# A two-layer decoder on one core: loads and weight splits of the first element reordered, the last batch's projection spread over its pairs, side work of the recurrence moved to other steps

## The chip, the cores and the metric

One core of a Trainium2 chip runs the whole program. TensorE multiplies into banks of PSUM (2 KB a partition), VectorE, ScalarE and GpSimd read and write SBUF, the first two PSUM as well; transfers are issued by the sync engine's queue (SP) and can be by ScalarE's. The metric is device microseconds from start to end of the program, median of the runs.

## The reference

Two decoder layers on x [8, 256, 128] with context [8, 512, 128]; after every sublayer the sum with x is normalised.

```python
x = ln(x + L0_attn(x))            # 16 heads of 8, causal, window 64, relative bias, softmax
x = ln(x + L0_xattn(x, ctx))      # 16 heads of 64, rotary keys, scores clipped at 11, softmax
x = ln(x + L0_ffn(x))             # weight rounded to -1, 0, 1; x scaled by its peak
x = ln(x + L1_attn(x))            # recurrence over 256 tokens
x = ln(x + L1_xattn(x, ctx, ctx, mask))   # linear attention
x = ln(x + L1_ffn(x))             # fp8-rounded x and weight

def step(state, inp):             # the recurrence of L1_attn
    u_t, sp_t = inp
    state = jnp.tanh(state @ A.T + u_t @ B.T) + sp_t
    return state, state @ C.T
```

## The kernel before

Each engine has one program, written out in order; semaphores tie them. The order is by hand: a step that waits holds all that stands behind it on its engine.

**First element** (start to line 2032 on TensorE). The loads (lines 501 to 540) are issued by SP one after the other. `rel`, the relative bias, is transposed, copied to `rel_row`, written to a DRAM scratch (line 513) and read back as `bias_mask`, four transfers (line 519). `x`, `w_qkv` and `w_proj` (`w_nat`) are transposed; `q0`, `k0`, eight masked copies `km` and `vm` follow. Scores of eight head pairs (`first_scores`, `first_score`, line 1251) go through two pairs of banks; ScalarE takes the exponentials (`exps_of`, line 867); probabilities are turned by TensorE in twelve jobs, even ones copied by ScalarE (`even_turn`), odd ones by VectorE (`odd_turn`, line 1321), and weighed into `o0`, which VectorE divides (`S_DIVIDE`, line 1271). `S_PROJ` makes y, `S_X1` x1, `S_LATN` the latents `lat`, `S_LAT` their split. Beside it the context is turned (`ctx_t`), normalised (`cn`), turned and split; its key/value products (`products_of_ctx`) are measured (`measure_kv`) and scaled (`keep_kv`). cos and sin are spread and turned (`prepare_trig`, `keep_cos`, `sin_t`).

fp32 products of the cross-attention are made from a high and a low part of each operand. The weights are split once: ScalarE copies the high part (`split_high`, lines 925 to 933), GpSimd subtracts it (`split_low`, line 697), four weights of 1024 columns. TensorE waits for all of them before the first keys.

**Batches.** Eight batches of eight head pairs. In a pair: scores in two units (line 2133), exp, clamp on VectorE (line 1471), `values_of` (line 2057), sums of the four exp tiles on GpSimd (lines 731 to 735), `sum_of` (line 2065), reciprocal and product on VectorE (`attended`, lines 1373 and 1374), and GpSimd's `rotate` of the keys (line 641). Keys, queries and values of later pairs are made by jobs whose PSUM bank `number_jobs` gives: "p" and a second bank by `SECOND_BANK`, in turns; pair 3 has none, so all its jobs go through "p". In batches 0 to 6 the self-attention of the next batch runs in slots between. In the last batch `beside_last_batch` prepares the tail's matrices and each batch's f (`normalize_f`, `turn_f`, `keep_f`); the output projection of the last batch stands behind it (lines 2189 to 2205).

**Tail and recurrence.** f is quantised, multiplied, x3 normalised in four parts (`add_product`, `normalize_x3`). Two are turned and give the first 64 steps of z (`begin_z`); the others are made beside the recurrence (`late_work`), as is the rest of z in thirds from step `LATE_Z` on. A step is 2 x 2 matmuls of 8 columns and a tanh. Windows of 16 steps carry the following sublayers (`window`; on VectorE `rectify_queries`, line 1584). Steps that have nothing else get a `keep_clock` matmul of 192 or 96 columns.

## Time and profile before

| | us |
|---|---|
| runs: lowest, median, highest of 3 | 1046.6, 1050.55, 1050.72 |
| profiled execution | 1047.62 |
| its span, first to last instruction | 1045.9 |
| first element | 0 to 57.9 |
| eight batches | 57.9 to 812.1 |
| tail before the recurrence | 812.1 to 839.7 |
| recurrence, 255 steps | 839.7 to 988 |
| rest | 988 to 1045.9 |

TensorE is busy 88% of the span, VectorE 65%, ScalarE and GpSimd 49% each. The mean granted TensorE clock is 0.944; a clock of 0.5 in a stretch is 1.2 GHz, one of 1.00 is 2.4 GHz. The shares are averages over stages with different limits; a saving is read from the waits inside a stage.

### The profile page before, as it was taken

The page shows a single profiled execution, that of the slowest core. Times are in us where ns is not written, and L with a number is a line of the kernel's source. Part 1 is how long each engine was busy: PE and PEld are TensorE (multiplying, and loading weights), DVE is VectorE, ACT ScalarE, POOL GpSimd, SP SyncE. Part 2 cuts the span into 40 slices and gives each one's busy share as a digit, 9 for nine tenths or more (in the row PEclk, how much of TensorE's full clock was granted, in tenths as well). Part 3 has the DMA queues.
Part 4 walks back from the last instruction along what each step waited for, and adds up shares of the span by engine and source line. Part 5 has one row for each costly group of instructions (what it writes and reads, how often), then busy time and mean ns, then how long its engine had stood idle before and what let it go on. Part 6 is the DMA issues. An engine that isn't in the chain of part 4 may idle for free.

```text
span 1045.9 us, 22097 instructions
## 1 busy us (share of the span) xinstructions
PE 919.8 (88%) x8504; PEld 652.6 (62%) x8504; DVE 681.3 (65%) x1906; ACT 509.6 (49%) x1441; POOL 510.7 (49%) x642
## 2 busy tenths in 40 slices
PE   6689989998999999899989999998988499999922
PEld 4456656666665756566666666666656379888721
DVE  6446577568757766776687577667689543444477
ACT  6655645653663556456636645564233023333324
POOL 2643475356546534654565466446657112333363
PEclk9989999999999989999999999999999589999955
DMA  7000000000000000000000000000000001222211
...
DMA packets 60470, 15.09 MB, mean 14 GB/s; under 512 B 41278, under 2 KB 59726, under 8 KB 60238
## 3 DMA queue, kind: packets, MB, share of 16 engines
...
q14 instruction: 36, 0.29, 0.1%
...
## 4 chain that ended last, share of the span: by engine, by line
PE 64%; DVE 19%; ACT 7%; POOL 5%; issue 3%; DMA 1%; SPq 0%; POOLq 0%; DVEq 0%; ACTq 0%
PE score_banks L2133 10%; PE out_bank L2057 8%; PE score_banks L1758 5%; DVE o_rec L1373 5%; PE bank_a L1753 5%; PE score_banks L2071 4%; DVE prob L1471 3%; PE score_banks L1789 3%; PE score_banks L1760 3%; PE score_banks L1759 3%; PE score_banks L2261 3%; PE bank_d L1774 3%; PE out_bank L2040 2%; PE out_bank L2065 2%; PE bank_d L2274 2%
## 5 line engine op out<-in xcount | busy, mean ns | idle before, releaser
L1007 ACT ACTIVATE prob<-score_banks 128x1024 f32<-128x1024 f32 x128 | 131.0, 1024 | 165.8 <-PE score_banks L2133 165.5
L733 POOL TENSOR_TENSOR psum<-psum,prob 128x512 f32<-128x512 f32 x64 | 81.6, 1275 | 153.9 <-DVE prob L1471 153.9
L2133 PE MATMUL score_banks<-qh,kr 64*128 64x256 f32 x1024 | 150.9, 415 | 2.1 <-ACT qh L916 1.3
L731 POOL TENSOR_TENSOR psum<-prob 128x512 f32<-128x512 f32 x64 | 82.6, 1290 | 98.4 <-DVE prob L1471 98.3
L1373 DVE RECIPROCAL o_rec<-out_bank 128x256 f32<-128x256 f32 x64 | 111.9, 1748 | 26.1 <-PE out_bank L2065 26.0
L2057 PE MATMUL out_bank<-prob,v 128*64 128x256 f32 x1024 | 124.7, 386 | 1.4 <-DVE on L1374 1.4
L2133 PEld LDWEIGHTS score_banks<-qh,kr 64*128 64x128 f32 x1024 | 91.9, 193 | 40.7 <-issue 30.5
L867 ACT ACTIVATE prob<-prob,neg_max 128x128 f32<-128x128 f32 (+1 forms) x256 | 107.1, 426 | 13.5 <-DVE neg_max L1258 13.5
L1471 DVE TENSOR_SCALAR prob<-prob 128x1024 f32<-128x1024 f32 x128 | 101.4, 792 | 12.9 <-ACT prob L1007 12.9
L2057 PEld LDWEIGHTS out_bank<-prob,v 128*64 128x64 f32 x1024 | 67.9, 136 | 46.6 <-issue 17.2
L1056 ACT ACTIVATE prob<-score_banks 128x8 f32<-128x8 f32 x255 | 45.1, 177 | 96.1 <-PE score_banks L2261 96.1
L1315 DVE TENSOR_TENSOR k_cos<-score_banks,cos_t 128x512 f32<-128x512 f32 x56 | 38.2, 682 | 72.4 <-PE score_banks L1760 46.2
L641 POOL TENSOR_TENSOR kr<-k_cos,k_sin 128x512 f32<-128x512 f32 x64 | 82.8, 1294 | 4.4 <-DVE k_sin L1317 3.6
L735 POOL TENSOR_TENSOR psum<-psum,prob 128x512 f32<-128x512 f32 x64 | 81.6, 1275 | 3.9
L2261 PE MATMUL score_banks<-prob,pt 128*64 128x8 f32 x1020 | 74.3, 210 | 0.6 <-ACT prob L1053 0.3
L835 ACT ACTIVATE pt<-bank_a 128x512 f32<-128x512 f32 x84 | 50.2, 598 | 35.5 <-PE bank_a L1753 34.6
L1774 PE MATMUL bank_d<-km,q 64*128 64x128 f32 x480 | 50.6, 330 | 17.9 <-DVE row_max L1253 16.6
L2261 PEld LDWEIGHTS score_banks<-prob,pt 128*64 128x64 f32 x1020 | 53.4, 137 | 20.8 <-ACT prob L1056 14.5
L2071 PE MATMUL score_banks<-w_qkv_t,ident 128*64 128x96 f32 (+1 forms) x336 | 64.8, 277 | 0.0
L1753 PE MATMUL bank_a<-ident,prob 128*128 128x128 f32 x360 | 57.0, 281 | 4.0 <-ACT pt L835 2.3
L1789 PE MATMUL score_banks<-pt,vm 128*32 128x128 f32 x768 | 54.0, 281 | 4.5 <-ACT pt L938 3.8
L760 POOL TENSOR_TENSOR var_eps<-mv,epsilons 128x1 f32<-128x1 f32 x49 | 9.5, 194 | 96.1 <-DVE mv L1575 96.1
...
## 6 DMA issues: line engine op xcount, KB each, us to landing
...
```

Of the source, the lines that this page charges most:

```text
L641: g.tensor_tensor(kr[:, key % 2, :], k_cos[:, :], k_sin[:, :], ALU.add).then_inc(kr_ready, 1)
L731: link(g.tensor_tensor(psum[:, p % 2, :], pp[:, 0, :], pp[:, 1, :], ALU.add))
L867: last = s.activation(pr, pr, ACT.Exp, bias=neg_max[:, qt, j, g:g + 1], accum_out=row_sum[:, qt, j, g:g + 1])
L1007: s.activation(prob[:, p % 2, 2 * u:2 * u + 2, :].rearrange("p k (h q) -> p h k q", h=2), sc[:, 0:2, :].rearrange("p h (k q) -> p h k q", ...
L1373: link(w.reciprocal(o_rec[:, :], bank[:, T:2 * T]))
L1471: w.tensor_scalar(pr, pr, float(np.exp(-CLIP)), float(np.exp(CLIP)), ALU.max, ALU.min).then_inc(clamped, 1)
L1753: return nc.tensor.transpose(out_ap, in_ap, ident[0:in_ap.shape[0], 0:in_ap.shape[0]])
L1789: last = mm(o0_bank[32 * g:32 * g + 32, qt * P:(qt + 1) * P], vm[:, kt, j, 32 * g:32 * g + 32], pt[:, t % 2, i * P:(i + 1) * P], start=(j ...
L2057: mm(o[DH * h:DH * (h + 1), 0:T], v[:, (q // 2) % 2, kb, lo:lo + DH], prob[:, q % 2, kb, T * h:T * (h + 1)], start=(kb == 0), stop=(kb == ...
L2071: mm(bank[0:HALF_ROWS, 0:columns], ident[:, 0:HALF_ROWS], w_qkv_t[:, 0:columns], start=True, stop=True, skip_group_check=True)
L2133: last = mm(sc[:, h, k * T:(k + 1) * T], kr[rows_of, p % 2, kb * P:(kb + 1) * P], qh[rows_of, p % 2, :], start=True, stop=True, skip_group ...
L2261: last = mm(cf[lo:lo + HALF_ROWS, t * B:(t + 1) * B], a_t[:, lo:lo + HALF_ROWS], hid[:, (t - 1) * B:t * B], start=False, stop=True, skip_g ...
```

## The change

In the first element: the identity is made first and TensorE waits for it alone; w_qkv and w_proj are issued by ScalarE; the scratch write and its read-back come before most loads, cos and sin behind the large weights; the high parts of all weights and the low parts of `wq` and `wv` are made by VectorE, the keys' low parts by GpSimd; TensorE waits for the keys' parts before keys and for the others before values; first jobs use five banks; scores run ahead of the context's work, and the key/value sum ahead of the second values. `prob1`'s zeros are written by GpSimd, `ctx_t` by VectorE. In the last batch all second banks are "o0"; the output of pair p - 2 is added up in pair p; the last two adds of the last pair's sum are VectorE's. Ahead of the recurrence the second part of x3 is turned into its own bank before z begins. In the recurrence the late products start at step 9 and 18 instead of 3 and 10, the late turns at 26 and 42 instead of 17 and 25, and z's thirds go to the steps of `Z_STEPS`; VectorE's late parts move accordingly, and keep_clock follows whether a step carries work.

```diff
+FIRST_BANKS = ("p", "d2", "s0", "s1", "o", "p", "s0")
 SECOND_BANK = ("o0", "o0", "o0", None, "d2", "d2", "o0", "o0")
...
+bank = fixed or (second if second and bank == "p" else "p")
...
-        add((b, p, kind), kind, target, SECOND_BANK[p])
+        add((b, p, kind), kind, target, SECOND_BANK[p] if b < B - 1 else "o0")
...
+LAST_D2_JOB = [j.done for j in JOB.values() if j.bank == "d2"][-1]
+FIRST_LATE = 9
+Z_EARLY = (13, 14, 15, 22, 30, 38, 46, 54, 58, 60, 61, 62)
+Z_STEPS = [*Z_EARLY, *(t for t in range(64, T) if t % WINDOW_STEPS in (10, 12, 13, 14))][:3 * Z_PARTS]
-    load(w_nat[:, 0:3, :], a["L0_attn_w_qkv"].rearrange("(k p) c -> p k c", p=P), signal=qkv_in)
-    load(w_nat[:, 3, :], a["L0_attn_w_proj"], signal=qkv_in)
...
+    sp.wait_ge(d_free, 1)
+    sp.dma_start(scratch, rel_row).then_inc(scratch_out, 16)
+    row("L0_attn_b_proj", b_proj, signal=proj_in)
...
     col("L0_xattn_ln_ctx_b", CTX_B, signal=ctx_cols_in)
...
     sp.wait_ge(scratch_out, 16)
+    load(keep[:, :, :], a["mask_BxS2_ff1"].rearrange("b (k p) -> p b k", p=P), slow=True, signal=keep_in)
     load(wkv_nat, a["L0_xattn_Wkv"], signal=split_in)
     load(wq_nat, a["L0_xattn_Wq"], signal=split_in)
+    load(trig_nat[:, 0], a["L0_xattn_cos"].rearrange("(k p) d -> p k d", p=P), signal=trig_in)
+    load(trig_nat[:, 1], a["L0_xattn_sin"].rearrange("(k p) d -> p k d", p=P), signal=trig_in)
+    link(g.memset(ident[:, :], 0.0))
+    g.affine_select(out=ident[:, :], in_=ident[:, :], compare_op=ALU.not_equal, fill=1.0, base=0,
+                    pattern=[[-1, P]], channel_multiplier=1).then_inc(ident_ready, 1)
...
+    g.memset(prob1[:, :, 0:WINDOW], 0.0).then_inc(zeros_ready, 1)
+        last = split_low(1, low, wkv_nat[:, 0:INNER].rearrange(swapped, t=2, d=HALF)[:, 1 - t], high)
+    last.then_inc(keys_split, 1)
-    split_low(2, wq_s[:, 1, :], wq_nat, wq_s[:, 0, :])
-    split_low(3, wv_s[:, 1, :], wkv_nat[:, INNER:2 * INNER], wv_s[:, 0, :]).then_inc(weights_split, 1)
...
+            if pair == B * PAIRS - 1:
+                first.then_inc(last_sum_begun, 1)
+                break
...
+        if k == 1:
+            rstd_of(NORMS, 3, 4, EPS_LN, half=1)
+    act.dma_start(w_nat[:, 0:3, :], a["L0_attn_w_qkv"].rearrange("(k p) c -> p k c", p=P)).then_inc(qkv_in, 16)
+    act.dma_start(w_nat[:, 3, :], a["L0_attn_w_proj"]).then_inc(qkv_in, 16)
...
-    act.wait_ge(ctx_full, 1)
-    s.activation(ctx_t[:, :], bank_p[:, :], ACT.Identity).then_inc(ctx_kept, 1)
-    act.wait_ge(trig_full, 2)
-    s.activation(sin_t[:, :], sc[:, 1, :], ACT.Identity, scale=sign[:, 0:1]).then_inc(sin_kept, 1)
     apply_norm(0).then_inc(cn_ready, 1)
+    exps_of(0, 0, 0, 1)
+    exps_of(0, 1, 0, 2)
+    even_turn(0)
     act.wait_ge(ctx_cols_in, 16 * 2)
     act.wait_ge(cn_full, 1)
...
-    exps_of(0, 0, 0, 1)
-    keep_kv(0, 0)
-    exps_of(0, 1, 0, 2)
-    even_turn(0)
+    s.activation(cn_raw_first[:, :], bank_p[:, :], ACT.Identity, **by_feature)
+    s.activation(cn_s[:, 0, 0, :], bank_p[:, :], ACT.Identity, **by_feature).then_inc(cn_kept, 1)
     exps_of(0, 1, 1, 2)
     even_turn(2)
-    split_high(0)
     exps_of(0, 2, 0, 2)
     even_turn(4)
     exps_of(0, 2, 1, 2)
-    split_high(1)
+    keep_kv(0, 0)
     exps_of(0, 3, 0, 2)
     even_turn(6)
     exps_of(0, 3, 1, 2)
+    act.wait_ge(trig_full, 2)
+    s.activation(sin_t[:, :], bank_d2[:, :], ACT.Identity, scale=sign[:, 0:1]).then_inc(sin_kept, 1)
+    even_turn(8)
     keep_kv(0, 1)
-    even_turn(8)
-    split_high(2)
     even_turn(10)
-    split_high(3)
...
-                    bank_a[:, :].rearrange("p (b t) -> p b t", b=4))
+                    (bank_a, ob)[k][:, :].rearrange("p (b t) -> p b t", b=4))
+        dve.wait_ge(split_in, 16 * 2)
+        if part == 0:
+            last = w.tensor_copy(wk_s[:, 0, :], wkv_nat[:, 0:INNER])
+        if part == 1:
...
+    def split_low(part):
+        dve.wait_ge(weights_high, part + 1)
+        full, t = ((wq_nat, wq_s), (wkv_nat[:, INNER:2 * INNER], wv_s))[part - 2]
+        w.tensor_tensor(t[:, 1, :], full, t[:, 0, :].bitcast(F32), ALU.subtract).then_inc(weights_split, 1)
...
-    prepare_trig()
-    centre_weights()
-    keep_cos()
-    dve.wait_ge(scratch_out, 16)
-    w.memset(prob1[:, :, 0:WINDOW], 0.0)
-    measure_kv(0, 0)
+    dve.wait_ge(ctx_full, 1)
+    w.tensor_copy(ctx_t[:, :], bank_p[:, :]).then_inc(ctx_kept, 1)
     for at in range(6):
         first_score(at)
     odd_turn(1)
     first_score(6)
     first_score(7)
+    centre_weights()
     odd_turn(3)
+    measure_kv(0, 0)
+    split_high(0)
+    split_high(1)
+    odd_turn(5)
+    prepare_trig()
+    self_attention(0, S_CN, 0)
+    split_high(2)
+    odd_turn(7)
+    keep_cos()
     measure_kv(0, 1)
-    odd_turn(5)
-    self_attention(0, S_CN, 0)
-    odd_turn(7)
+    split_high(3)
+    split_low(2)
     odd_turn(9)
     invert_sums(0)
     odd_turn(11)
     self_attention(0, S_DIVIDE, 0)
+    split_low(3)
     self_attention(0, S_PROJ, 0)
     first_keys("a", 0)
+    self_attention(0, S_RELU, 0)
     self_attention(0, S_X1, 0)
     first_keys("b", 0)
     self_attention(0, S_LATN, 0)
     first_keys("a", 1)
     self_attention(0, S_LAT, 0)
-    self_attention(0, S_RELU, 0)
     first_keys("b", 1)
     self_attention(0, S_KV_SUM, 0)
...
+            def add_last_sums():
+                dve.wait_ge(last_sum_begun, 1)
+                dve.wait_ge(clamped, 2 * pair + 2)
+                link(w.tensor_tensor(psum[:, p % 2, :], psum[:, p % 2, :], prob[:, p % 2, 2, :], ALU.add))
+                w.tensor_tensor(psum[:, p % 2, :], psum[:, p % 2, :], prob[:, p % 2, 3, :],
+                                ALU.add).then_inc(last_sum_ready, 1)
...
-    add_product(0)
-    add_product(1)
+    measure_x3(0, *add_product(0))
+    measure_x3(1, *add_product(1))
     normalize_x3(0)
     normalize_x3(1)
     quantize_f(2)
     quantize_f(3)
-    add_product(2)
-    normalize_x3(2)
-    add_product(3)
+    measure_x3(2, *add_product(2))
...
         if k == 1:
+            normalize_x3(2)
+            product_3 = add_product(3)
+        if k == 2:
             normalize_x3(3)
-            keep_late(0)
...
         normalize_window(W_Q, q1, bank_d[:, 0:D]).then_inc(q_ready, 1)
+        if k == 2:
+            keep_late(1)
         if k == 1:
-            keep_late(1)
+            measure_x3(3, *product_3)
+            keep_late(0)
-    first_scores(0)
-    pe.wait_ge(kv_centred, 1)
+    for at in range(3):
+        first_scores(at)
     pe.wait_ge(ctx_kept, 1)
-    products_of_ctx(0, bank_p)
-    first_scores(1)
     pe.wait_ge(cn_ready, 1)
     for k in range(KB):
-        last = turn(ob[:, k * P:(k + 1) * P], cn[:, k, :])
+        last = turn(bank_p[:, k * P:(k + 1) * P], cn[:, k, :])
     last.then_inc(cn_full, 1)
-    for at in range(2, 6):
+    for at in range(3, 6):
         first_scores(at)
+    pe.wait_ge(zeros_ready, 1)
...
+    first_turn(3)
+    first_weigh(2)
+    pe.wait_ge(kv_centred, 1)
+    pe.wait_ge(cn_kept, 1)
+    products_of_ctx(0, bank_p)
+    for at in range(4, 7):
+        first_turn(at)
+        first_weigh(at - 1)
+    pe.wait_ge(trig_ready, 1)
+    pe.wait_ge(d_free, SETUP_D + D_SCORE + 7)
+    for t, bank in enumerate((bank_d, bank_d2)):
+        for k in range(KB):
+            last = turn(bank[:, k * P:(k + 1) * P], trig_rep[:, t, k].rearrange("p r d -> p (r d)"))
+        last.then_inc(trig_full, 1)
+    first_turn(7)
+    first_weigh(6)
     pe.wait_ge(kv_free, 1)
     products_of_ctx(1, bank_p)
-    for at in range(3, TURNS):
+    for at in range(8, TURNS):
         first_turn(at)
         first_weigh(at - 1)
...
-    pe.wait_ge(weights_split, 1)
+    pe.wait_ge(keys_split, 1)
     pe.wait_ge(cn_split, 1)
     pe.wait_ge(kv_free, 2)
     prep_keys(JOB["keys a", 0], 0, "a")
+    pe.wait_ge(cos_kept, 1)
     self_attention(0, S_PROJ)
+    pe.wait_ge(sin_kept, 1)
     prep_keys(JOB["keys b", 0], 0, "b")
-    for half in range(2):
-        prep_values(JOB[f"values {half}", 0], 0, half)
-    prep_keys(JOB["keys a", 1], 0, "a")
-    prep_keys(JOB["keys b", 1], 0, "b")
+    pe.wait_ge(weights_split, 2)
+    pe.wait_ge(d_free, SETUP_D + D_SCORE + 8)
+    prep_values(JOB["values 0", 0], 0, 0)
+    self_attention(0, S_KV_SUM)
+    prep_values(JOB["values 1", 0], 0, 1)
     pe.wait_ge(weights_in, 16 * SETUP_LOADS)
     pe.wait_ge(lat_ready, 1)
     for qt in range(QT):
         last = turn(bank_a[:, qt * P:(qt + 1) * P], lat[:, qt, :])
     last.then_inc(a_full, 1)
+    pe.wait_ge(odd_free, TURNS // 2)
+    prep_keys(JOB["keys a", 1], 0, "a")
+    prep_keys(JOB["keys b", 1], 0, "b")
     pe.wait_ge(lat_split, 1)
     prep_queries(JOB["queries", 0], 0)
-    self_attention(0, S_KV_SUM)
...
     def beside_last_batch(p):
+        if p == 2:
+            engine, count = LAST_D2_JOB
+            pe.wait_ge(p_free[engine], count)
+        if p >= 2:
+            output_of_last(p - 2)
...
     values_of(B * PAIRS - 1)
+    sum_of(B * PAIRS - 1)
+    output_of_last(PAIRS - 2)
+    turn_f(B - 2)
+    output_of_last(PAIRS - 1).then_inc(y_full, 1)
...
-            last = turn(bank_a[:, i * P:(i + 1) * P], x3_tok[k][:, i, :])
+            last = turn((bank_a, ob)[k][:, i * P:(i + 1) * P], x3_tok[k][:, i, :])
+    turn_x3(0)
+    turn_x3(1)
     begin_z(0)
     begin_z(1).then_inc(c_ready, 1)
-        for k, first in ((2, 3), (3, 10)):
+        worked = False
+        for k, first in ((2, FIRST_LATE), (3, FIRST_LATE + 9)):
...
-        for k, first in ((2, 17), (3, 25)):
+        for k, first in ((2, 26), (3, 42)):
...
-        if LATE_Z <= t < LATE_Z + 3 * Z_PARTS:
-            part, third = divmod(t - LATE_Z, 3)
+        if t in Z_STEPS:
...
         if not worked:
-            keep_clock(KEEP_Z if busy else KEEP, spare)
-        elif not busy and i not in (0, 6):
+            keep_clock(KEEP_Z if worked_late or t < FIRST_LATE else KEEP, spare)
+        elif i not in (0, 6) and t > WINDOW_STEPS:
             keep_clock(KEEP_Z, spare)
```

## Rows read from the trace of the kernel before

**Rows 1.** Stages: length, busy us and instructions by engine, then PEclk, DMA, GB/s.
```profile
0.00:57.90 57.90, 37.91 (x291) 26.59 (x291) 32.10 (x144) 35.11 (x109) 24.84 (x51) 0.97 0.38 97
...
812.10:839.70 27.60, 14.73 (x45) 10.21 (x45) 14.05 (x54) 2.79 (x4) 4.22 (x8) 0.51 0.00 0
839.70:846.30 6.60, 6.41 (x64) 5.85 (x64) 1.21 (x4) 1.51 (x9) 0.00 (x0) 0.50 0.01 2
```

**Rows 2.** Timeline, bias: start, us, engine, line, operation; landing of `bias_mask`.
```profile
5.87 0.43 SPq L513 DMA_DIRECT2D bias_scratch<-prob  x1
...
8.95 1.87 SPq L519 DMA_DIRECT2D bias_mask<-bias_scratch  x1
...
DMA to landing us min/median/max: 4.7/5.4/6.1
...
16.18 0.26 DVE L1251 CUSTOM_DVE_ANT_0 prob<-bank_d,bias_mask 128x128 f32<-128x128 f32 x1
```

**Rows 3.** Chain of waits, end of the weight splits: start us, us, engine, line.
```profile
39.05 0.95 ACT wq_s L931
...
42.40 2.35 POOL wv_s L697
```

**Rows 4.** Timeline, from `o0` to the first unit; in brackets idle time before.
```profile
42.80 0.42 DVE L1271 TENSOR_TENSOR o<-score_banks,rec_t 128x256 f32<-128x256 f32 x1 [0.81 <-PE score_banks L1789]
46.25 0.42 DVE L1276 TENSOR_TENSOR y<-bank_d,xbp 128x256 f32<-128x256 f32 x1 [3.03 <-PE bank_d L1880]
...
51.08 0.60 DVE L1190 TENSOR_SCALAR lat<-x,mv,rstd 128x128 f32<-128x128 f32 x2 [0.51 <-POOL rstd L626]
...
54.17 0.60 PE L1753 MATMUL bank_a<-ident,lat 128*128 128x128 f32 x2
...
56.86 1.10 PE L1888 MATMUL bank_d<-v,k 128*128 128x130 f32 x8
```

**Rows 5.** Two lines, last batch: ns min/median/max, starts; then the cn split.
```profile
L1190 DVE TENSOR_SCALAR lat<-x,mv,rstd x8: 342/1161/1423, 752.0 to 804.5; 128x128 f32<-128x128 f32 x8
...
L1471 DVE TENSOR_SCALAR prob<-prob x15: 674/682/684, 739.6 to 803.6; 128x1024 f32<-128x1024 f32 x15
...
31.46 0.68 DVE L1305 TENSOR_TENSOR cn_s<-k_sin,cn_s 128x512 fp32r<-128x512 f32 x1
```

**Rows 6.** Timeline, TensorE in pairs 1 and 3 of the last batch.
```profile
752.17 0.38 PE L1758 MATMUL score_banks<-wv_s,cn_s 128*128 128x256 f32 x1 [0.88 <-DVE k_sin L1317]
...
769.39 0.38 PE L1758 MATMUL score_banks<-wv_s,cn_s 128*128 128x256 f32 x1 [1.16 <-DVE k_sin L1317]
...
772.77 2.08 PE L2133 MATMUL score_banks<-qh,kr 64*128 64x256 f32 x8
```

**Rows 7.** Timeline, end of the last batch, TensorE and VectorE.
```profile
805.64 3.39 PE L2196 MATMUL bank_d<-wo,on 128*128 128x128 f32 x28
...
809.88 1.76 DVE L1373 RECIPROCAL o_rec<-out_bank 128x256 f32<-128x256 f32 x1 [0.53 <-PE out_bank L2065]
```

**Rows 8.** Timeline, x3 to z, TensorE.
```profile
831.17 1.12 PE L1753 MATMUL bank_a<-ident,cb 128*128 128x128 f32 x4 [3.42 <-DVE cb L1190]
...
837.56 1.22 PE L2238 MATMUL score_banks<-prob,pt 128*128 128x256 f32 x2 [1.17 <-ACT prob L990]
```

**Rows 9.** Timeline, tanh steps on ScalarE: steps 4, 26 and 32 of the recurrence.
```profile
842.62 0.18 ACT L1056 ACTIVATE prob<-score_banks 128x8 f32<-128x8 f32 x1 [0.78 <-PE score_banks L2261]
...
857.00 0.18 ACT L1056 ACTIVATE prob<-score_banks 128x8 f32<-128x8 f32 x1 [1.02 <-PE score_banks L2261]
...
861.16 0.18 ACT L1056 ACTIVATE prob<-score_banks 128x8 f32<-128x8 f32 x1 [0.59 <-PE score_banks L2261]
```

**Rows 10.** Timeline, first window of the recurrence: VectorE, then the first attend on TensorE.
```profile
857.57 0.41 DVE L1578 TENSOR_SCALAR psum<-bank_d,mv,rstd 128x128 f32<-128x128 f32 x1 [0.94 <-POOL rstd L762]
...
860.09 0.41 DVE L1584 TENSOR_SCALAR psum<-bank_a,cols 128x128 f32<-128x128 f32 x1 [0.56 <-PE bank_a L2269]
...
861.52 0.39 PE L2297 MATMUL out_bank<-psum,km 128*64 128x16 f32 x8
```

136 lines of the change are left out of this document (63 added, 73 removed).

## The prediction

> **What bounds the kernel now.** I read the busy shares first, then the stages, then the chain of waits inside each stage that the change touches, then the single instructions on it. No engine is the bound over the whole span; the stretches have different limits, and the change edits four of them.
>
> The first element runs from 0 to 57.9 us, with TensorE busy only 37.9 us of it [rows 1]. Its chain starts with the bias table: the scratch row is written at 5.87, read back as `bias_mask` from 8.95, landed 4.7 to 6.1 us after each issue, and the first score is read at 16.18 [rows 2]. It goes on with the splitting of weights: ScalarE's copy for `wq_s` (0.95 us), then GpSimd's 2.35 us for `wv_s`, before which TensorE starts no keys [rows 3]. `o0` is divided at 42.80, y waits 3.03 us for its product, `lat` is ready at 51.7, and its transpose starts at 54.17, queued behind values and keys; 1.10 us of key/value sum stand directly ahead of the first unit at 57.9 [rows 4].
>
> The seven batches from there to 742 are hardly touched. In the last batch pair 3 has all its projections in bank "p" in a row: TensorE stands still 1.16 us for `k_sin` and falls to the low clock, so that the next unit takes 2.08 us for its 8 matmuls [rows 6]. From 812.1 to 839.7 TensorE is at 0.51 of its clock and waits for the other engines [rows 1]. The recurrence is ScalarE and TensorE in turns: 255 steps in the 148.3 us from 839.7 to 988. A plain step is 0.565 us, its 0.18 on ScalarE and 0.39 of waiting; 255 of them would be 144.1, so 4.2 us are lost in a few steps (three of them in [rows 9]).
>
> **The change part by part.** The sum is made against the profiled execution: 1047.62 us, of which the span is 1045.9. The median of the three runs is 1050.55, 2.9 us higher; the saving is taken to be the same for both.
>
> *First element, head.* `ident` comes first on GpSimd, w_qkv and w_proj are issued from ScalarE's queue (two issues, 0.43 us each by the SP rows), and the scratch write moves ahead of eight issues, so it goes out at about 3.6 instead of 5.87 [rows 2]. The read-back follows 3.1 us later as before, at 6.7, and lands at 11.4 to 12.8. VectorE's work ahead of the scores, now with the `ctx_t` copy but without trig, weight centring, memset and first key/value statistics, ends near 11. The first score is then read at 12.0, 4.2 us earlier, and all exponentials move up by as much.
>
> *First element, splits.* ScalarE loses four copies of 1024 columns, VectorE gets them. SBUF to SBUF with one source it takes 0.68 us for 1024; with two sources 0.68 for 512 [rows 5]. I take 0.68 each (one source, both sides in SBUF) and keep 1.36 as the upper bound; the two low parts taken from GpSimd have two sources, 1.2 to 1.4 us each. From its first key/value statistics (ending at 26.6 by this schedule) to the division VectorE now has four turn evacuations (2.4), trig (0.7), the cn split (0.6), four high parts (2.7), one low part (1.2), cos (0.6), statistics (1.3) and the inversion (1.8): 11.3 us, and some 2.2 us in which it waits for TensorE's order: 40.1. VectorE, not the splits on GpSimd, is the new bound here.
>
> What adds to that is the neighbour. The 128-column normalisations of `lat` take 342 ns alone and up to 1423 ns while GpSimd adds [rows 5]: such a pass waits for a GpSimd instruction to end. GpSimd's low parts of the keys (two of 2.35 us [rows 3]) now run beside prepare_trig and the high parts. Between nothing and 3.2 us are lost, so the division lies between 40.1 and 43.3; I take 42.2, two thirds of the way, since only the seven one-source passes can be held and three or four of them meet a long GpSimd instruction. The Trainium skill (SBUF — State Buffer, "SBUF: two separate sides") says that VectorE's two-port passes, and also its passes with two sources in SBUF against a GpSimd instruction that reads SBUF, shut each other out for a whole instruction. The first half agrees with the 342 and 1423 ns. By the second half the moved low parts would be held too, the division would come at 43.3 and the total be 1.1 us higher.
>
> From the division to the first unit the kernel takes 57.9 - 42.8 = 15.1 us. The wait of y (3.03) is replaced by the last low part (1.2), since the product now finds its weights: -1.8. The 2.5 us in which `lat` waits behind values and keys go, and the sum of 1.10 us moves ahead of it; but `kr` for pair 0 and the next k_cos now stand before the split of `lat` on VectorE: +0.7. That leaves 10.4 [rows 4]. Saving of the stage: 4.7, and 0.6 from the earlier division: **5.3 us**; bounds 3.0 (all passes held, and once more behind the division) and 7.4.
>
> *Last batch.* With two banks in pair 3 the first values need not wait for `k_sin`, only the second, as in pair 1, where the wait is 0.88 us [rows 6]. The second values then end 2.3 us earlier. The output matmuls, 28 in 3.39 us [rows 7], cost 0.46 us a pair: on the path in pair 3, which leaves 1.9, and in pair 5 (0.46 more), hidden in the even ones, where GpSimd's adds and rotate end later than TensorE. Without the low clock the unit takes 1.13 rather than 2.08, which wins up to 0.95; I take it whole. The 3.39 us that leave the end save nothing by themselves: the last reciprocal waited only 0.53 us for TensorE [rows 7], so VectorE was free at 809.35. It now does the last two adds (1.36 us) and wins 0.93 where GpSimd no longer holds its normalisation: free at 809.8, no gain. Stage: 1.9 + 0.95 - 0.46 - 0.2 = **2.2 us**, the 0.2 being what is hidden less than fully; bounds 1.0 and 3.2.
>
> *Between batch and recurrence.* The first x3 transpose starts at 831.17 and the second half of z only at 837.56, since transpose and copy of the second half stand between; the first tanh comes at 839.7 [rows 8]. With a bank of its own the second transpose runs beside the first copy and ends at 833.8, then both halves of z follow at 2.07 us each: 838.0. **1.6 us**, bounds 1.2 and 1.8.
>
> *Recurrence.* Four steps with side work at the low clock last 0.96 us, the others there 0.67. Moving it to step 9 saves 4 x 0.29 = 1.2 us, less if the clock rises later than 6.4 us after the first step. The step with 1.02 us of idle (waiting for x3) becomes a plain one: 0.64. Three window starts that carry z as well lose 0.22 each (0.59 idle for 0.39), five smaller ones 0.2 together [rows 9]. Against it: behind the first q (normalised at 857.98) VectorE has statistics of x3 (1.25), keep_late (1.0) and the w8 copy (0.15) ahead of rectify_queries (1.06): 861.45. The first attend started at 861.52, 0.35 us behind its input; with 0.64 and 0.22 less before it, it would start at 860.66 and so stalls 0.8 [rows 10]. 1.2 + 0.64 + 0.65 + 0.2 - 0.8 = **1.9 us**; bounds 0.8 and 2.9.
>
> The sum: 5.3 + 2.2 + 1.6 + 1.9 = **11.0 us**. That is 1036.6 for the profiled execution and 1039.5 from the median; I predict 1038.
>
> **The rivals.** *VectorE is held throughout.* Every one-source pass beside GpSimd's splits waits, the first element saves 1 to 3 us: total 6 to 8, about 1042. For it the 1423 ns; against it that such passes are seven in a stretch of 15 us. By the skill's page above this is the rule rather than the exception.
>
> *Nothing is held.* GpSimd's splits fall between VectorE's passes: division at 40.1, and the clock rises early in the recurrence: 14 to 15 us, 1034.
>
> *Slower: the recurrence stays at the low clock.* Steps 1 to 8 now hold one 96-column keep_clock beside the 8-column matmuls and no side work; in the kernel before the clock rose right after the four steps that had it [rows 1, 9]. At the low clock a plain step costs 0.10 us more, one with side work 0.40. Of the first 64 steps 29 carry side work: 3.5 + 11.6 = 15.1 us, 2.0 of them paid today. The forecast holds 0.8 of it (eight steps). The gain of 11 is used up if the clock stays low to about step 50 (0.236 a step); if it stays so to step 100, with four side steps in sixteen, 36 x 0.175 = 6.3 come on top: 21.4, and 1038 + 20.6 = 1059. Against it: in the steps before the side work TensorE had no idle rows either.
>
> *The banks or the lifted order don't do what they say*: VectorE or GpSimd holds pair 3 anyway and the first unit waits for `rotate`; last batch and first element give under 2 us together: 1046, no change.
>
> **How the numbers follow.** Forecast (total 8.5 to 13): 0.50. VectorE held: 0.20. Nothing held: 0.13. Banks and order without effect: 0.12. Clock low past step 50: 0.05. Range 1030 to 1046: it takes in the first three cases, with the 2.9 us between profile and median on either side, and leaves out most of the last two. 0.5%, about what a measurement of this kernel can tell from no change, is 5.3 us: faster than 1045.3 holds 0.50 + 0.19 + 0.13 = 0.82; the same 0.13; slower 0.05.
>
> **What would show it.** First score near 12 us, division at 40 to 43, first unit at 51 to 54; a high part near 0.7 us alone and over 1.5 us beside GpSimd. In pair 3 no idle of over 1 us but one, and the next unit at 1.1 us; the last reciprocal released by VectorE itself. Both x3 transposes before the first z. From first unit to first tanh 778.0 us where it was 839.7 - 57.9 = 781.8. Steps 3 to 6 at 0.67 us, one longer step at 34. I am wrong if the first unit starts after 55.5, or if steps after the twelfth last 0.67 us or more.

## The result and the profile after

The changed kernel takes 1038.67 us, the median of five runs (1037.42 to 1040.2); the kernel before, run beside it, 1048.51 (1046.6 to 1050.72, five runs). The ratio is 0.9905, with a 95% interval of 0.9884 to 0.9926. The profiled execution took 1038.29 us, 9.3 less than that of before.

I cut both profiled executions at the same instructions, among them the reciprocals of the attention sums (one for each pair of each batch), and set the difference beside the forecast:

| stretch (us) | before | after | difference | forecast |
|---|---|---|---|---|
| start to reciprocal of pair 0, first batch | 76.40 | 71.72 | -4.68 | -5.3 |
| to reciprocal of pair 0, last batch | 672.31 | 672.88 | +0.57 | 0 |
| to reciprocal of pair 7, last batch | 61.17 | 58.87 | -2.30 | -2.2 |
| to the first tanh | 29.78 | 27.37 | -2.41 | -1.6 |
| first to last tanh | 148.34 | 147.78 | -0.56 | -1.9 |
| to the end | 57.90 | 57.88 | -0.02 | 0 |
| sum | 1045.90 | 1036.50 | -9.40 | -11.0 |

So the time is close to the 1038 forecast. The table alone doesn't say that the reasons hold; for the first row, they turned out not to. That row also reaches further than its forecast, which was made for the first unit of the cross-attention's scores: there the difference is 3.10 us (57.90 to 54.80). The other 1.58 arise in the next four microseconds, as these rows show, two from the kernel before and one from the changed one:

```profile
57.90 1.98 PE L2133 MATMUL score_banks<-qh,kr 64*128 64x256 f32 x8
60.40 0.63 PE L1759 MATMUL score_banks<-cn_s,wk_s 128*128 128x512 f32 x1
...
56.20 0.39 PE L1801 MATMUL score_banks<-cn_s,wk_s 128*128 128x512 f32 x1
```

The kernel before runs this stretch at half clock (58.0 to 61.4 us), the changed one doesn't; its first unit, shown below, takes 1.13 us.

The stages of the changed kernel (length, busy us and instructions of each engine, PEclk, DMA share, GB/s), to be read beside [rows 1]: before the recurrence TensorE is still at half its clock, and in its first ten microseconds it is again for most of the time.

```profile
0.00:54.80 54.80, 38.70 (x291) 28.16 (x291) 39.88 (x154) 30.31 (x102) 23.78 (x50) 0.97 0.41 102
54.80:738.00 683.20, 639.03 (x4844) 433.15 (x4845) 466.50 (x1208) 377.54 (x955) 364.60 (x373) 0.98 0.02 5
...
805.30:830.84 25.54, 14.29 (x45) 10.35 (x45) 14.42 (x54) 2.79 (x4) 4.21 (x8) 0.51 0.00 0
830.84:840.70 9.86, 9.29 (x100) 7.86 (x101) 0.93 (x2) 2.48 (x14) 0.00 (x0) 0.65 0.01 2
```

The timeline of the first element in the changed kernel, the rows that answer [rows 2, 4, 5]: first score, the split of cn and the cast of `wq_s`, GpSimd's subtractions beside them, division, y, first unit.

```profile
12.68 0.29 DVE L1249 CUSTOM_DVE_ANT_0 prob<-bank_d,bias_mask 128x128 f32<-128x128 f32 x1 [1.14 <-PE bank_d L1816]
...
29.70 2.84 DVE L1303 TENSOR_TENSOR cn_s<-k_sin,cn_s 128x512 fp32r<-128x512 f32 x1
32.46 1.75 DVE L1341 CAST wq_s<-prob 128x1024 fp32r<-128x1024 f32 x1
...
29.45 2.54 POOL L707 TENSOR_TENSOR wk_s<-prob,wk_s 128x1024 fp32r<-128x1024 f32 x1
31.95 3.40 POOL L707 TENSOR_TENSOR wkx_s<-prob,wkx_s 128x512 fp32r<-128x512 f32 x2
...
43.33 0.42 DVE L1269 TENSOR_TENSOR o<-score_banks,rec_t 128x256 f32<-128x256 f32 x1 [2.17 <-PE score_banks L1831]
...
45.66 0.42 DVE L1274 TENSOR_TENSOR y<-bank_d,xbp 128x256 f32<-128x256 f32 x1 [0.77 <-PE bank_d L1922]
...
54.80 1.13 PE L2201 MATMUL score_banks<-qh,kr 64*128 64x256 f32 x8 [0.56 <-ACT qh L936]
```

The first score moves up by 3.5 us, but the division comes 0.53 later than before: all that was won ahead of it is lost again in between (0.54 of it to half clock from 42.0 to 45.4 us, as the late bias below shows). The split of cn takes 2.84 us where it took 0.68.

From the last batch and the way to z, the rows that answer [rows 6, 8] (the last reciprocal, [rows 7], starts at 803.47 with no idle time in front):

```profile
765.29 0.38 PE L1800 MATMUL score_banks<-wv_s,cn_s 128*128 128x256 f32 x1 [0.72 <-DVE k_sin L1315]
...
824.92 1.12 PE L1795 MATMUL bank_a<-ident,cb 128*128 128x128 f32 x4 [3.42 <-DVE cb L1188]
826.44 1.12 PE L1795 MATMUL out_bank<-ident,k 128*128 128x128 f32 x4 [0.41 <-DVE k L1188]
827.35 1.12 PE L2297 MATMUL score_banks<-prob,pt 128*128 128x256 f32 x2
```

And from the recurrence, ScalarE's tanh instructions that answer [rows 9]: tanh 6, behind a plain step at half clock; tanh 10, behind one with side work; tanh 35, behind step 34, which waits for the first attend.

```profile
834.33 0.18 ACT L1053 ACTIVATE prob<-score_banks 128x8 f32<-128x8 f32 x1 [0.49 <-PE score_banks L2322]
...
837.29 0.18 ACT L1053 ACTIVATE prob<-score_banks 128x8 f32<-128x8 f32 x1 [0.78 <-PE score_banks L2322]
...
853.46 0.18 ACT L1053 ACTIVATE prob<-score_banks 128x8 f32<-128x8 f32 x1 [0.98 <-PE score_banks L2322]
```

### The profile page after: what moved, and what is told of

The parts are those of the page before. It is cut to its first block, busy times and chain, and to the rows that moved or that the text cites. A ratio compares the mean times of both kernels' runs of the same rounds, so it can differ in the third digit from the quotient of the medians.

```text
span 1036.5 us, 22193 instructions
## 1 busy us (share of the span) xinstructions
PE 916.3 (88%) x8550; PEld 657.1 (63%) x8550; DVE 689.3 (66%) x1915; ACT 505.2 (49%) x1434; POOL 507.1 (49%) x639
## 4 chain that ended last, share of the span: by engine, by line
PE 62%; DVE 21%; ACT 7%; POOL 5%; issue 4%; DMA 1%; POOLq 0%; SPq 0%; DVEq 0%; ACTq 0%
PE score_banks L2201 9%; PE out_bank L2110 8%; DVE o_rec L1400 5%; PE score_banks L1800 5%; PE bank_a L1795 4%; DVE prob L1498 4%; PE score_banks L2127 3%; PE score_banks L2322 3%; PE score_banks L1831 3%; PE bank_d L1816 3%; PE score_banks L1801 3%; PE score_banks L1802 3%; PE out_bank L2093 2%; PE bank_d L2335 2%; PE out_bank L2121 2%
## 5 line engine op out<-in xcount | busy, mean ns | idle before, releaser
L1004 ACT ACTIVATE prob<-score_banks 128x1024 f32<-128x1024 f32 x128 | 131.1, 1024 | 164.7 <-PE score_banks L2201 164.4
L750 POOL TENSOR_TENSOR psum<-psum,prob 128x512 f32<-128x512 f32 x63 | 80.2, 1273 | 152.9 <-DVE prob L1498 152.9
L752 POOL TENSOR_TENSOR psum<-psum,prob 128x512 f32<-128x512 f32 x63 | 80.3, 1275 | 3.8
L2127 PE MATMUL score_banks<-w_qkv_t,ident 128*64 128x96 f32 (+1 forms) x336 | 60.7, 264 | 0.0
L930 ACT ACTIVATE v<-score_banks 128x512 f32<-128x512 f32 x57 | 34.0, 596 | 46.0 <-PE score_banks L1802 45.2
```

What stands on the lines that cost most here:

```text
L1004: s.activation(prob[:, p % 2, 2 * u:2 * u + 2, :].rearrange("p k (h q) -> p h k q", h=2), sc[:, 0:2, :].rearrange("p h (k q) -> p h k q", ...
L2127: mm(bank[0:HALF_ROWS, 0:columns], ident[:, 0:HALF_ROWS], w_qkv_t[:, 0:columns], start=True, stop=True, skip_group_check=True)
```

## The experiments

All are edits of the changed kernel. Since executions of one kernel differ by 2 to 8 us, more than most single parts are worth, I read their traces at the cuts of the table; the medians stand beside them, and no median by itself decides between two of these edits, but for the fillers. Each reading is of one profile. For the first element I count from the first score to the reciprocal of pair 0, because the first score itself moves between 12.0 and 12.7, most of it with TensorE's speed ahead of it. The same first scores, in the changed kernel and in the first run below:

```profile
11.09 1.44 PE L1816 MATMUL bank_d<-km,q 64*128 64x128 f32 x8 [0.62 <-DVE vm L1238]
...
11.04 0.82 PE L1822 MATMUL bank_d<-km,q 64*128 64x128 f32 x8 [0.83 <-DVE vm L1232]
```

1.44 us is what these eight products also take in a recorded stretch at half clock (267.33 us in the changed kernel). PEclk shows 1.00 here in both profiles, so the half clock at the start of the program has to be read from the length of the products. In seven of the changed orders' profiles the products take 0.82 us and the first score comes at 11.99 to 12.39; in six, the changed kernel's among them, they take 1.44 and it comes at 12.53 to 12.70.

**Low parts of the keys on VectorE.**

```diff
-            split_low(0, wk_s[:, 1, :], wkv_nat[:, 0:INNER], wk_s[:, 0, :])
...
-                last = split_low(1, low, wkv_nat[:, 0:INNER].rearrange(swapped, t=2, d=HALF)[:, 1 - t], high)
...
             split_high(3)
-            split_low(2)
+            split_low(0)
+            split_low(1)
...
+            split_low(2)
             split_low(3)
```

> The changed kernel with the low parts of the key weights (one of 1024 columns, two of 512 in swapped order) on VectorE too, so that GpSimd subtracts nothing in the first element; VectorE does them behind the high part of the values, and the low part of the queries moves behind the division. Changed kernel: cn split 2.84 us, cast of wq_s 1.75 us, division 43.33, first unit 54.80, reciprocal of pair 0 at 71.72. Theory (VectorE's passes are held by GpSimd's subtractions): cn split 0.7 and cast 0.7, which gives back 3.2 us; 2.6 us of new subtractions take part of it, 1.2 of which is paid back by the moved query part: division near 41.5, y about 44.3, pair 0 near 70.3, total 1.4 us lower. Rival (they are held by something else, such as the weights' DMA or ScalarE): both stay at 2.8 and 1.8, division near 44.7, total 1 to 2 us higher.

Measured: 1039.79 us (ratio to before 0.9932, 0.9902 to 0.9961). The passes on VectorE's timeline:

```profile
29.02 0.68 DVE L1297 TENSOR_TENSOR cn_s<-k_sin,cn_s 128x512 fp32r<-128x512 f32 x1
29.63 0.68 DVE L1335 CAST wq_s<-prob 128x1024 fp32r<-128x1024 f32 x1
...
41.35 0.42 DVE L1263 TENSOR_TENSOR o<-score_banks,rec_t 128x256 f32<-128x256 f32 x1 [0.73 <-PE score_banks L1837]
```

The holding is GpSimd's: 2.84 and 1.75 become 0.68 and 0.68. Division, y and pair 0 came at 41.35, 43.96 and 69.66, close to what was expected. But of the 2.06 us at pair 0, 0.67 is the earlier first score, and 1.24 a stretch at half clock (42 to 45.5 us) which this profile lacks and that of the changed kernel has. From the first score to pair 0 it is 57.65 us, against 57.80 in a profile of the changed kernel's order without such a stretch (the kernel of the late bias, below). The 3.23 us given back pay for the added subtractions and for waits on TensorE (0.53 and 1.46 us), and no more: 0.15 of the 1.4 expected.

**Memsets in place of GpSimd's subtractions.**

```diff
-                return g.tensor_tensor(low, full, high.bitcast(F32), ALU.subtract)
+                return g.memset(low.bitcast(F32), 0.0)
```

> The changed kernel in which GpSimd's three subtractions for the low parts of the keys are memsets of the same tiles: the low parts of the keys are left out of the computation, and GpSimd reads no SBUF there. Theory (a GpSimd instruction that reads SBUF holds VectorE's passes): cn split and wq_s cast about 0.7 us each, division about 40.5 to 41.5, since the last turns and the inversion follow VectorE. Rival (any GpSimd instruction holds them): a pass that meets a memset takes up to 1.6 us. Rival (not GpSimd): 2.84 and 1.75 stay. First unit by the theory 2 to 3 us earlier than 54.80, total 1035.5 to 1037 by the median.

Measured: 1038.29 us (0.9921, 0.9893 to 0.9949); division 41.13, first score to pair 0 56.73 us, without a stretch at half clock; that is 1.07 less than 57.80, the length with the subtractions and no such stretch. GpSimd's and VectorE's timeline:

```profile
28.83 0.95 POOL L707 MEMSET wk_s<- 128x1024 f32 x1
29.72 1.26 POOL L707 MEMSET wkx_s<- 128x512 f32 x2
...
28.42 2.10 DVE L1144 COPY v<-v 128x512 f32<-128x512 f32 x2
30.44 0.67 DVE L1303 TENSOR_TENSOR cn_s<-k_sin,cn_s 128x512 fp32r<-128x512 f32 x1
31.03 0.68 DVE L1341 CAST wq_s<-prob 128x1024 fp32r<-128x1024 f32 x1
```

The theory was half right. The split of cn, two sources in SBUF, runs in 0.67 us beside the second memset, though a subtraction held it for 2.2 us. The copy of one source ahead of it takes 2.10 us for its two instructions instead of 0.75: a memset holds that one. So what GpSimd does decides which passes it holds. The Trainium skill (SBUF — State Buffer, "SBUF: two separate sides") states just this pair of rules: one-source copies in the two-port mode exclude any GpSimd access, two-source passes only a GpSimd instruction that reads SBUF. Both halves agree with these rows.

**The bias later.** First behind five issues more on SP's queue, then behind nine.

```diff
-            sp.wait_ge(d_free, 1)
-            sp.dma_start(scratch, rel_row).then_inc(scratch_out, 16)
             row("L0_attn_b_proj", b_proj, signal=proj_in)
...
+            sp.wait_ge(d_free, 1)
+            sp.dma_start(scratch, rel_row).then_inc(scratch_out, 16)
             sp.wait_ge(scratch_out, 16)
```

> The changed kernel with the scratch write of the bias behind five more issues on SP's queue (b_proj, the two key/value weights, two columns), as it was in the kernel before: 2.3 us later. Theory (VectorE's queue of work carries a later first score to the division): first score near 15.0 instead of 12.68, division 45.3 to 45.7, pair 0's reciprocal 2 to 2.3 us later, total 2.2 us up. Rival (the division is set by the held passes and GpSimd's statistics, so that the early bias is worth nothing): division within 0.5 us of 43.33, total unchanged.

Measured: 1038.05 us (0.9905, 0.9878 to 0.9932). The write moved by 1.2 us only, since SP had waited for its row until 3.5 us anyway; first score 12.67, division 42.79, pair 0 70.47. This profile has no stretch at half clock in the first element, and so gives its undisturbed length: 57.80 us from first score to pair 0 (57.81 in the profile of the outputs at the end, which has none either). The second kernel:

> The changed kernel with the scratch write of the bias behind nine more issues on SP's queue, 3.6 us later than now, and its read-back as well. (One us later left the first score at 12.67: TensorE's product, not the bias, was last.) Now the bias lands near 15, as in the kernel before (16.1). Theory (VectorE's queue carries it on, less the 1.7 us in which it waits between 13 and 26): first score 15 to 16, division 44.0 to 44.8 where it is 42.8 without a stretch of low clock, pair 0's reciprocal 71.5 to 72.5 instead of 70.5. Rival (nothing of the early bias reaches the division): 42.8 and 70.5.

Measured: 1039.3 us (0.9902, 0.9875 to 0.9929); write at 6.62, read-back at 8.61, nearly as late as in the kernel before (8.95), and the first score:

```profile
12.39 0.29 DVE L1249 CUSTOM_DVE_ANT_0 prob<-bank_d,bias_mask 128x128 f32<-128x128 f32 x1 [0.53 <-PE bank_d L1816]
```

Still 12.39, and it waits for TensorE. First score to pair 0 is 58.93 us, with one stretch at half clock, where the changed kernel has 59.04, with one too. Both theories had the first score later and were wrong in that: with the read-back only 0.34 us ahead of its old place, the score still waits for TensorE, so loading the bias first brings nothing here. VectorE's timeline in the kernel before shows what held it there:

```profile
13.08 0.69 DVE L1165 COPY cos_t<-score_banks 128x512 f32<-128x512 f32 x1
13.93 0.91 DVE L1337 MEMSET prob<- 128x1024 f32 x1 [0.16 <-issue]
14.95 0.89 DVE L1176 BATCH_NORM_STATS2 stats<-score_banks 128x6 f32<-128x128 f32 x4
15.88 0.38 DVE L1179 BATCH_NORM_AGGREGATE mv<-stats 128x2 f32<-128x6 f32 x4
```

From 10.00 to the first score at 16.18 VectorE works with one pause of 0.16 us and waits for no load. The 3.5 us come from the other work that the change takes from in front of the scores: from 11.20 to 16.18 all is such work, and the copy of `ctx_t` that comes in its place takes 0.68.

**Low parts of queries and values back on GpSimd.**

```diff
             self_attention(0, S_KV_SCALE[1], 0)
+            split_low(2, wq_s[:, 1, :], wq_nat, wq_s[:, 0, :])
+            split_low(3, wv_s[:, 1, :], wkv_nat[:, INNER:2 * INNER], wv_s[:, 0, :]).then_inc(weights_split, 2)
...
-            split_low(2)
...
-            split_low(3)
```

> The changed kernel with the low parts of the query and value weights back on GpSimd, behind the second key/value scale, and the high parts still on VectorE. Theory (they are off the path either way, since TensorE starts the values only at 46.2): GpSimd ends them at 44.2, y is not behind a subtraction on VectorE any more, division 42.5 to 43 without a stretch at half clock (43.3 with one), pair 0's reciprocal within 0.7 us of 70.5 (71.7 with one). Rival (taking them from GpSimd was what made the first element faster): GpSimd's affine of the keys and the root for y come 4.7 us later, pair 0's reciprocal at 73 or later.

Measured: 1037.22 us (0.9891, 0.9861 to 0.9921); division 41.33, pair 0 at 69.71, 57.64 us behind the first score with one stretch at half clock: 1.4 us less than the changed kernel's 59.04. Better than the theory, and the opposite of the rival. Of the 1.4 us, 0.86 lie ahead of the division, which comes 29.26 us behind the first score here and 30.12 in the late bias, neither with a recorded stretch at half clock in between; the rest assumes that one stretch at half clock costs the same in both profiles. GpSimd does the two in time it has to spare, while VectorE's subtraction for the queries (1.22 us) stands on the path to the division. The one behind the division costs less: in the changed kernel VectorE still waits 0.77 us for TensorE after it.

```profile
37.96 2.35 POOL L707 TENSOR_TENSOR wq_s<-prob,wq_s 128x1024 fp32r<-128x1024 f32 x1
40.26 2.37 POOL L707 TENSOR_TENSOR wv_s<-prob,wv_s 128x1024 fp32r<-128x1024 f32 x1
```

**Pair 3 of the last batch with one bank.**

```diff
-                add((b, p, kind), kind, target, SECOND_BANK[p] if b < B - 1 else "o0")
+                add((b, p, kind), kind, target, SECOND_BANK[p] if b < B - 1 or p == 3 else "o0")
```

> The changed kernel with pair 3 of the last batch using bank p alone, as before. From reciprocal of pair 2 to that of pair 3: 12.18 us in the kernel before, 9.41 in the changed one. Theory (the second bank takes away the wait for k_sin): 9.41 + 1.9 = 11.3 us, 12.2 if TensorE also falls to half its clock there; total 1.9 to 2.8 up. Rival (the gain came from VectorE's last sums or from the output products' new places): it stays at 9.4.

Measured: 1040.45 us (0.9914, 0.9887 to 0.9941). From pair 2 to pair 3 11.13 us, against 9.41: the second bank is worth 1.72. The other 1.05 of the 2.77 is the half clock, which this profile doesn't have there, less what the output product in this pair costs. TensorE's waits in the pair:

```profile
764.06 0.50 PE L1800 MATMUL score_banks<-cn_s,wkx_s 128*128 128x512 f32 x1 [0.85 <-ACT qh L936]
...
765.81 0.39 PE L1800 MATMUL score_banks<-wv_s,cn_s 128*128 128x256 f32 x1 [0.78 <-DVE k_sin L1315]
...
767.47 0.39 PE L1800 MATMUL score_banks<-wv_s,cn_s 128*128 128x256 f32 x1 [0.69 <-ACT v L930]
```

**The output products at the end again.**

```diff
-                if p >= 2:
-                    output_of_last(p - 2)
...
-            sum_of(B * PAIRS - 1)
-            output_of_last(PAIRS - 2)
+            for p in range(PAIRS - 1):
+                output_of_last(p)
             turn_f(B - 2)
+            sum_of(B * PAIRS - 1)
```

> The changed kernel with the output products of the last batch at its end, ahead of the last sums, as before; the last two sums stay on VectorE. Theory (28 products cost 0.46 us in pairs 3 and 5, where TensorE is last; at the end they are hidden behind VectorE, which is busy until 803.5, nearly wholly): pair 3 8.95 us instead of 9.41, pair 5 8.07 instead of 8.53, last pair 8.3 to 8.9: total 0.9 lower to 0.3 lower. Rival (the 3.4 us in a row at the end delay the last sums): last pair 8.29 + 2 or more, total 1 to 2.5 us higher.

Measured: 1037.56 us (0.9892, 0.9855 to 0.9929). Pairs 3 to 7 take 9.24, 8.13, 8.08, 7.18 and 8.44 us, together 41.07; in the changed kernel 9.41, 8.23, 8.53, 7.18 and 8.29, together 41.64. Spreading the products costs 0.57 us: 0.45 in pair 5, 0.17 in pair 3, where half a microsecond was expected in each, and 0.10 in pair 4, with 0.15 won back in the last.

**x3 through one bank.**

```diff
-                    last = turn((bank_a, ob)[k][:, i * P:(i + 1) * P], x3_tok[k][:, i, :])
+                    last = turn(bank_a[:, i * P:(i + 1) * P], x3_tok[k][:, i, :])
...
             turn_x3(0)
+            begin_z(0)
             turn_x3(1)
-            begin_z(0)
             begin_z(1).then_inc(c_ready, 1)
```

> The changed kernel with both x3 transposes through bank_a, the second behind the first half of z, as before. From the last reciprocal to the first tanh: 29.78 us before, 27.37 in the changed kernel, where 1.6 of it was forecast for this edit. Theory (the edit is all of it, its size was underestimated because z's first half starts beside the second transpose): 29.5 to 29.9. Rival (0.8 of the 2.4 comes from elsewhere, such as the clock rising before the first step): 28.8 to 29.1.

Measured: 1041.59 us (0.9925, 0.9887 to 0.9963); last reciprocal to first tanh 29.95 us, 2.58 more than in the changed kernel. The edit accounts for the whole 2.41, and its size was underestimated.

**x3's statistics behind the queries.**

```diff
                 if k >= 2:
                     rectify_queries(k - 2)
+                if k == 2:
+                    measure_x3(3, *product_3)
+                    keep_late(0)
                 dve.wait_ge(pre_full, k)
```

> The changed kernel with the statistics of the last x3 part and the first keep_late behind rectify_queries of window 0 instead of ahead of it. Theory (these two, 2.3 us, make the first attend wait): the step at t = 34, now 1.15 us, becomes 0.57 to 0.70, and no other step grows: 0.5 us less from first to last tanh (147.78 now), total 0.5 lower, within the noise of the median. Rival (the wait goes elsewhere, to the window's x4 statistics, which now come behind them): step 34 is plain and a step between 35 and 42 grows by as much.

Measured: 1039.89 us (0.9922, 0.9891 to 0.9953). Step 34 is plain, 0.56 us; step 39 takes 1.38 instead of 0.56, since the transpose of x4 now waits for a normalisation that comes behind the 2.3 us:

```profile
857.27 0.44 PE L2331 MATMUL bank_a<-ident,v 128*64 128x128 f32 x4 [0.71 <-DVE v L1615]
...
857.99 0.18 ACT L1053 ACTIVATE prob<-score_banks 128x8 f32<-128x8 f32 x1 [1.21 <-PE score_banks L2323]
```

The rival was right: the wait only moves.

**192 columns in the first steps.**

```diff
-                    keep_clock(KEEP_Z if worked_late or t < FIRST_LATE else KEEP, spare)
+                    keep_clock(KEEP_Z if worked_late else KEEP, spare)
```

> The changed kernel with 192 instead of 96 columns in keep_clock in steps 1 to 8 of the recurrence. In the changed kernel the steps start at the full clock, it falls after step 5 (834 us), steps 6 to 9 last 0.67, the four with side work 0.96, and it rises behind these. Theory (the light steps let it fall): no fall, all of steps 1 to 16 at 0.56 to 0.58, first to last tanh 147.78 - 2.1 = 145.6 us. Rival (it falls on account of the idle time before the recurrence, whatever the steps hold): it falls at the same place, 147.8, and up to 0.1 more for each 192-column step at half clock.

Measured: 1036.76 us (0.9882, 0.9852 to 0.9913); first to last tanh 145.65 us. The first 16 steps all last 0.56 to 0.57, the four with side work too; the one that ends here lasted 0.96 in the changed kernel:

```profile
835.50 0.18 ACT L1053 ACTIVATE prob<-score_banks 128x8 f32<-128x8 f32 x1 [0.39 <-PE score_banks L2322]
```

The theory holds: the 96-column steps let the clock fall. The end took 1.0 us longer (58.87). The clock falls 4.1 us behind the last tanh here, 8.9 in the changed kernel, and by the statistics that follow the first products at half clock (5.70 us behind the last tanh, for 5.03) that accounts for 0.67 of it.

**TensorE's idle time in the batches filled.**

```diff
+FILL_SUM, FILL_SCORE = 6, 5
...
+                    if at == 1:
+                        a_job(A_CN + 1)
+                        for _ in range(FILL_SCORE):
+                            mm(bank_a[0:DH, 0:T], ident[:, 0:DH], w_qkv_t[:, 0:T], start=True, stop=True,
...
+                if q == PAIRS - 2:
+                    for _ in range(FILL_SUM):
+                        mm(ob[0:DH, T:2 * T], ident[:, 0:DH], w_qkv_t[:, 0:T], start=True, stop=True,
```

> The changed kernel with idle TensorE time in the batches filled: five 64x256 matmuls that nobody reads into bank_a ahead of the wait for the scores of slot 8 (2.07 us idle), six into the free half of the output bank ahead of the wait for the last partial sums in pair 6 (2.39 us idle). In the changed kernel's profile TensorE runs at half its clock six times between 60 and 740 us, for 3.4 or 6.8 us, each time behind one of these two waits; batches measured from pair 1 to pair 1 last 95.2 us without such a stretch and 96.5 to 98.3 with it. Theory (idle TensorE time causes the stretches, and they are also what makes executions differ by up to 4 us): no stretch is left, every batch takes 95.2, reciprocal of pair 1 to that of the last batch's pair 0 652 us instead of 660.6, total 1030, executions within 2 us of each other. Rival (they come from something else than these waits): stretches stay, 660, total 1038 or more where the fillers run at half clock.

Measured: 1028.32 us (0.9801, 0.9769 to 0.9833). First the changed kernel, six batches from pair 1 to pair 1, then the one wait and the filler that takes its place, then two of the six batches with fillers:

```profile
84.00:179.20 95.20, 89.31 (x692) 60.64 (x694) 66.35 (x174) 53.55 (x136) 51.66 (x53) 1.00 0.02 5
179.20:277.10 97.90, 92.15 (x692) 62.50 (x692) 66.36 (x173) 53.65 (x136) 51.66 (x53) 0.97 0.02 5
277.10:373.90 96.80, 90.92 (x692) 61.39 (x694) 66.64 (x174) 53.53 (x136) 51.83 (x53) 0.98 0.02 5
373.90:469.10 95.20, 89.31 (x692) 60.64 (x694) 66.33 (x174) 53.55 (x136) 51.66 (x53) 1.00 0.02 6
469.10:565.60 96.50, 90.74 (x692) 61.79 (x694) 66.41 (x174) 53.65 (x136) 51.67 (x53) 0.98 0.02 5
565.60:663.90 98.30, 92.41 (x692) 62.98 (x694) 66.55 (x174) 53.76 (x136) 51.70 (x53) 0.97 0.01 4
...
527.46 0.65 PE L2121 MATMUL out_bank<-psum,ones 128*64 128x256 f32 x4 [2.39 <-POOL psum L752]
```

```profile
519.91 2.75 PE L2124 MATMUL out_bank<-w_qkv_t,ident 128*64 128x256 f32 x12
522.47 0.65 PE L2131 MATMUL out_bank<-psum,ones 128*64 128x256 f32 x4
...
178.40:273.60 95.20, 93.89 (x714) 63.52 (x714) 66.39 (x173) 53.45 (x136) 51.72 (x53) 1.00 0.02 6
273.60:368.80 95.20, 93.90 (x714) 63.53 (x714) 66.40 (x173) 53.45 (x136) 51.73 (x53) 1.00 0.02 5
```

Without fillers four batches of six are 1.3 to 3.1 us longer than 95.2, at a mean clock of 0.97 or 0.98 and with the same work in every other engine. With them all six last 95.2 at 1.00. From pair 1 to the last batch's pair 0 that is 652.06 us instead of 660.63. The theory holds for the batches. It doesn't for the executions, which still ranged from 1026.2 to 1031.8. In the last batch the fillers only cost: it takes 61.03 us for 58.87. They remove idle time and add columns at once, and no run separates the two.

**Three edits together**: the low parts of all weights on VectorE, the fillers (not in the last batch), 192 columns.

> The changed kernel with three edits at once: all low parts on VectorE; the idle time of TensorE in the batches filled, but not in the last batch, where the six fillers cost 2.5 us in front of pair 6's sums and gave 0.3 back; 192 columns in the first steps of the recurrence. Theory (the three add up): pair 0's reciprocal 69.7 (70.5 to 71 if a stretch at half clock falls into the first element), batches 95.2 each, last batch as in the changed kernel, first to last tanh 145.6, total 1024 (1028.3 less 2.2 for the last batch, 2.1 for the recurrence, 0.8 for VectorE, plus 0.9 for the tail, which grew when the recurrence was faster). Rival (the half clock removed in one place comes back in another, since it follows something other than idle time): 1029 or more.

Measured: 1027.89 us (1025.34 to 1028.27, ratio 0.9798, 0.9767 to 0.9829). Batches 652.06, first to last tanh 145.66 and the last batch 58.86, all as expected. Two parts weren't: pair 0 at 71.47, with a stretch at half clock in the first element and the first score at 12.70, and 59.71 from last tanh to the end, 1.8 us more than in the changed kernel. The clock now falls 4.4 us behind the last tanh, but that is 0.4 of it: `att_scratch` is written 6.64 us behind the last tanh for 6.24. It is read back 3.01 us later, where the changed kernel needs 1.54, and this transfer is the rest. Stage and transfer:

```profile
966.60:1026.30 59.70, 18.07 (x189) 12.70 (x185) 40.41 (x140) 18.59 (x43) 26.81 (x54) 0.54 0.13 27
...
973.23 0.32 SPq L585 DMA_DIRECT2D att_scratch<-on  x1
976.24 0.37 SPq L588 DMA_DIRECT2D prob<-att_scratch  x1
```

So it gives 1028 and not 1024, by the medians the same as the fillers alone: what the profile shows lost is a stretch at half clock in the first element and a slow transfer, and only 0.4 us is half clock that comes back behind the recurrence, as the rival had it. Its median is the lowest of all, 0.4 us below the fillers alone and 2% below the kernel before. The subtractions of queries and values, better left on GpSimd, were not tried in it.

## Why the prediction was right

**First element: the number near in part by luck, the reasons mostly wrong.** *Size.* The 5.3 us were forecast for the first unit, which gains 3.10, at the forecast's lower bound of 3.0. The 4.68 of the table is near 5.3 only because the kernel before ran at half clock just behind that unit and the changed one did not: 1.58 us that no term of the sum held. Half clock ahead of the unit blurs the 3.10 too. The changed kernel has one stretch there, which costs 1.24 us (54.80 against 53.56 in the late bias); the kernel before has one as well, from 51.2 to 54.6, which can have cost up to half of its 3.4 us. As an estimate from these figures, the change itself is worth 2.6 to 4.3 us at the first unit. The medians, over five executions each, differ by 9.8 us, which is why the total stands all the same; its division into stretches hangs on the two profiles.

*Head.* Forecast 4.2 us for the first score, measured 3.5; the missing 0.6 is the half clock at the start, since with the products at 0.82 us the first score comes at the forecast 12.0. But the cause put first, the bias table, is not it. The prediction read "landed 4.7 to 6.1 us after each issue, and the first score is read at 16.18" as a chain, with no row that showed VectorE idle in front of that score. There was none: it had no idle time. The work taken from VectorE, which the prediction names beside it, was the cause.

*Splits.* The division was forecast at 42.2 and came at 43.33, or 42.79 without a stretch at half clock. GpSimd holds VectorE for 2.16 us in the split of cn and 1.07 in the cast, 3.23 together: the upper bound of 3.2, not the two thirds that I took. The prediction excluded the two-source pass from being held, and by the section of the Trainium skill that it cited it should not have. The rival "VectorE is held throughout" was right in this term, and with it the first element was to save 1 to 3 us: the 3.10 at the first unit doesn't tell it from the forecast, and without the 1.58 the profiles would differ by 7.8 us in all, within that rival's 6 to 8 and below the forecast's 8.5 to 13.

*Behind the division.* From there to the first unit 11.47 us, or 10.77 in the profile of the late bias, where 10.4 was forecast. Moving query and value parts to VectorE, which I counted as a gain ("the product now finds its weights"), costs up to 1.4 us.

**Last batch: right in mechanism and sum.** Pair 3 gave 2.77 us where 1.9 + 0.95 was forecast. Its parts are off and cancel: the bank gave 1.72 where 2.3 was said, and the output product costs 0.17 there and not 0.46. Pair 5 lost 0.45, as forecast, and the last reciprocal waits for VectorE's own queue. The prediction saw that spreading the output products wins nothing by itself; the experiment gives 0.57 us as their price.

**x3 to z: mechanism right, size off.** 2.41 for 1.6, above the bound of 1.8. The sum let both halves of z follow the second transpose, 2 x 2.07 us; in the trace the first half starts at 827.35, while the second transpose is ending, and four products take 3.5 us.

**Recurrence: a term failed.** The step was "moving it to step 9 saves 4 x 0.29 = 1.2 us". The four steps still last 0.96 us: the clock, high at the start, falls in step 5 (833.9 us) and rises only with the side work, so that the first 16 steps take 11.30 us instead of 11.06. The rival "the recurrence stays at the low clock" had the mechanism, that light steps don't hold the clock; it was wrong on how long, since the side work raises it. The Trainium skill (TensorE: Matmul & The Clock Gate, "What's actually happening") says that the throttled state is the default and that activity releases it; the run with 192 columns agrees, with 2.1 us saved. The other terms held: the step that waited for x3 (1.20 us) is gone, the starts of three windows lost 0.22 each, and the new stall at step 34 is 0.58 where 0.8 was forecast.

**What the sum left out.** In the batches between, called "hardly touched", the changed kernel's profile is 0.57 us longer, from stretches at half clock that fall elsewhere in it. The prediction counted the clock only from the last batch on, and took the kernel before's stretches in the first element for work.
